# Attention loop of a post-LN layer: value bursts exchanged, the rounding of the maxima on GpSimd, one exponential per score tile

## What is computed

```python
Q = (x @ Wq.T + bq).reshape(b, t, 32, 16).transpose(0, 2, 1, 3)
K = (x @ Wk.T + bk).reshape(b, t, 8, 16).transpose(0, 2, 1, 3)
V = (x @ Wv.T + bv).reshape(b, t, 8, 16).transpose(0, 2, 1, 3)
Q, K = _rope(Q, K)
K, V = jnp.repeat(K, 4, axis=1), jnp.repeat(V, 4, axis=1)
w = jax.nn.softmax(jnp.einsum('bhqd,bhkd->bhqk', Q, K) / 4, axis=-1)
attn = jnp.einsum('bhqk,bhkd->bhqd', w, V)
x = _layernorm(x + attn.transpose(0, 2, 1, 3).reshape(b, t, 512) @ Wo.T + bo)
g = (x @ gate_w.T) * gate_s
u = (x @ up_w.T) * up_s
x = _layernorm(x + (silu(g) * u) @ down_w.T * down_s)
```

## Time and profile before

| | us |
|---|---|
| median of 3 executions | 1063.52 (1063.1 to 1064.48) |
| the profiled execution | 1064.13 |
| its span, first to last instruction | 1062.3 |

### The profile page before, as it was taken

How to read it: one execution, slowest core, us unless ns; L and a number is a source line. 1 busy time by engine, 2 the same in 40 slices (tenths; PEclk the granted TensorE clock), 3 DMA queues, 4 the chain that set the end, 5 groups by cost and what they waited for, 6 DMA issues and landing times.

```text
span 1062.3 us, 15699 instructions
## 1 busy us (share of the span) xinstructions
PE 1026.5 (97%) x5858; PEld 536.8 (51%) x5858; DVE 809.5 (76%) x1199; ACT 665.1 (63%) x1346; POOL 266.2 (25%) x227
## 2 busy tenths in 40 slices
PE   8999999999999999999999999999999999999996
PEld 3643344433443433443444443333337888888885
DVE  4899978899779799779988899999803475662535
ACT  2368877788778788778766678888863431222221
POOL 2751030141335422246200042844100000000002
PEclk9999999999999999999999999999999999999999
DMA  5274417243142512344140446531217510402011
GB/s 200 80 196 126 106 35 213 52 97 78 52 115 75 105 56 54 82 108 105 34 78 12 116 120 150 124 121 37 93 68 193 166 40 9 111 28 52 1 39 42
DMA packets 64432, 94.87 MB, mean 89 GB/s; under 512 B 37536, under 2 KB 37920, under 8 KB 62272
## 3 DMA queue, kind: packets, MB, share of 16 engines
q1 hardware_dynamic: 63776, 93.10, 33.2%
q10 hardware_dynamic: 576, 0.72, 0.2%
HBM read 53.95 MB, written 27.00 MB: 76 GB/s over the span
## 4 chain that ended last, share of the span: by engine, by line
PE 80%; DVE 10%; ACT 6%; issue 2%; DMA 1%; SPq 0%; POOL 0%; DVEq 0%; POOLq 0%
PE PS L448 21%; PE PV L467 20%; PE PSA L537 15%; PE PS L554 5%; PE PSA L426 5%; DVE nmx L964 5%; PE PS L365 4%; ACT Bn L756 3%; PE PS L493 2%; PE PSA L493 2%; DVE nmx L960 2%; DVE nmx L957 2%; ACT Bn L765 2%; PE PV L554 2%; PE PSA L365 1%
## 5 line engine op out<-in xcount | busy, mean ns | idle before, releaser
L756 ACT ACTIVATE Bn<-PS 128x512 f32<-128x512 f32 x1146 | 548.8, 559 | 125.0 <-PE PS L448 111.1
L448 PE MATMUL PS<-Qt,Kt 50*128 50x512 f32 x1146 | 391.7, 434 | 20.0 <-ACT Bn L756 18.7
L426 PE MATMUL PSA<-Kt,Qt 48*128 48x512 f32 x1024 | 390.0, 459 | 2.2 <-DVE Kt L936 0.8
L964 DVE TENSOR_REDUCE nmx<-PSA 128x1 f32<-128x1024 f32 x256 | 312.2, 1219 | 61.0 <-PE PSA L426 59.8
L448 PEld LDWEIGHTS PS<-Qt,Kt 50*128 50x128 f32 x1146 | 184.4, 184 | 323.6 <-ACT Bn L756 312.7
L467 PE MATMUL PV<-Bn 128*32 128x512 f32 x2048 | 272.8, 605 | 0.0
L426 PEld LDWEIGHTS PSA<-Kt,Qt 48*128 48x128 f32 x1024 | 174.6, 183 | 21.7 <-DVE nmx L964 6.2
L960 DVE TENSOR_REDUCE nmx<-PSA 128x1 f32<-128x512 f32 x256 | 174.5, 682 | 1.4 <-PE PSA L426 1.1
L957 DVE TENSOR_REDUCE nmx<-PSA 128x1 f32<-128x512 f32 x256 | 174.3, 681 | 0.0
L537 PE MATMUL PSA<-x1Th,wr 128*128 128x512 f32 x344 | 135.0, 393 | 0.8 <-DVE sg L1052 0.5
L537 PE MATMUL PSA<-x1Tl,wr 128*128 128x512 f32 x344 | 134.7, 392 | 0.0
(11 more groups left out here) (166 smaller groups left out, 919.4 us busy)
## 6 DMA issues: line engine op xcount, KB each, us to landing
Qt<-pscr SPq DMA_DIRECT2D x90, 128.0 KB, 4.9
A<-in_wf SPq DMA_DIRECT2D x11, 768.0 KB, 6.3
wr<-A SPq DMA_DIRECT2D x33, 256.0 KB, 2.9
pscr<-A SPq DMA_DIRECT2D x16, 512.0 KB, 3.7
vscr<-Bn SPq DMA_DIRECT2D x32, 256.0 KB, 2.0
Kt<-pscr SPq DMA_DIRECT2D x90, 64.0 KB, 2.3
A<-A SPq DMA_DIRECT2D x16, 256.0 KB, 3.7
Bn<-vscr SPq DMA_DIRECT2D x8, 512.0 KB
```

The lines of the kernel that those rows point to most:

```text
L426: op = e.matmul(PSA[:, 2 * s + h, :], Qt[n % 3][p:p + NC_, g % 2, 128 * qt:128 * qt + 128], Kt[n % 3][p:p + NC_, 512 * h:512 * h + 512], s ...
L448: e.matmul(PS2[:, i, cols], Kt[n % 3][rows, 128 * kt:128 * kt + 128], Qt[n % 3][rows, g % 2, 512 * qh + cols.start:512 * qh + cols.stop], ...
L756: e.activation(Pb[c % NP_][:, cols], PS2[:, score_bank[c, p], cols], ACT.Exp, scale=0.25).then_inc(*act_exp.next(piece(c, p)))
L964: e.tensor_reduce(nmx[:, hh % 2, c0:c0 + 1], slot_pair(s), AX.XY, ALU.max, negate=True).then_inc(*dve_max[s].next(k))
```

## The change

- The burst moves: `g == (3, 2)[u % 2]`, in an even unit behind S3/M3, in an odd unit behind S2/M2.
- The small piece is gone: every score tile is 512 columns, one product and one exponential, in bank c % 3.
- Background work stands behind the burst of its odd unit, so ahead of S3/M3 instead of behind it. ACT evacuates between the exponentials 2 and 3, and DVE does its part of it between the two half reductions.
- The maxima of half hh, for 1 <= hh < 31, are joined on DVE, rounded and split on GpSimd (`split_max`), and transposed on DVE behind the first reduction of the next half. `write_max` moves from the units v % 8 == 3 to v % 8 == 4 in SP's program.
- The row fetch `gather_at` moves to v == 5. The casts of a rotation move from the 6th and 7th unit behind the projection to the 7th and 9th, which are even units, and the write from the 8th to the 10th.

```diff
-        gather_at = {(n, {0: 13, 6: 5}.get(n, 3)): n + 2 for n in range(NG - 2)}
+        gather_at = {(n, {0: 13}.get(n, 5)): n + 2 for n in range(NG - 2)}
...
-            u0 = 16 * at_u[0] + at_u[1] + 6
-            rope_end.update({divmod(u0, 16): (j, "h0"), divmod(u0 + 1, 16): (j, "h1"), divmod(u0 + 2, 16): (j, "out")})
+            u0 = 16 * at_u[0] + at_u[1] + 7
+            rope_end.update({divmod(u0, 16): (j, "h0"), divmod(u0 + 2, 16): (j, "h1"), divmod(u0 + 3, 16): (j, "out")})
...
+        def apart(hh):
+            return 1 <= hh < 2 * NG - 1
+        def low_max(hh):
+            return (pool_ms if apart(hh) else dve_ms).at(("low", hh))
...
-            return [slice(0, 128), slice(128, 512)] if c % 8 == 3 and c < 4 * SPLIT else [slice(0, 512)]
...
                     scores(u, g)
                     advance(1)
-                    if len(pieces(4 * u + g)) == 2:
-                        scores(u, g, 1)
-                    if u >= 1 and g == (2, 3)[u % 2]:
+                    if u >= 1 and g == (3, 2)[u % 2]:
                         weigh(u - 1)
-                if at_u in project_at:
-                    for h, i in enumerate(free_banks(u)):
-                        project_half(project_at[at_u], h, i, (0, 1, 2, 3))
...
+                        background(u)
...
                 for g in range(4):
                     exponent(u, g)
+                    if g == 2 and at_u in project_at:
+                        for h, i in enumerate(free_banks(u)):
+                            evacuate_raw(project_at[at_u], h, i)
                 if u >= 1:
                     finish(u - 1)
-                if at_u in project_at:
-                    for h, i in enumerate(free_banks(u)):
-                        evacuate_raw(project_at[at_u], h, i)
...
+                if 1 in halves and k % 16 == 15:
+                    join_max(hh)
+                    if not apart(hh):
+                        split_max(hh)
+                        turn_max(hh)
+                if k % 16 == 0 and k > 16 and apart(hh - 1):
+                    turn_max(hh - 1)
...
+            def split_max(hh):
+                top = nmx[:, hh % 2, 0:16]
+                w.wait_ge(*dve_ms.at(("join", hh)))
+                w.wait_ge(*dve_ms.at(("turn", hh - 1)))
+                e.tensor_copy(msp[:, 0:16], top).then_inc(*pool_ms.next(("high", hh)))
+                w.wait_ge(*pool_ms.at(("high", hh)))
+                e.tensor_tensor(msp[:, 16:32], top, msp[:, 0:16].bitcast(F32), ALU.subtract).then_inc(
+                    *pool_ms.next(("low", hh)))
...
+                if u % 8 == 3 and apart(steps_done(u) // 16 - 1):
+                    split_max(steps_done(u) // 16 - 1)
                 if at_u in project_at:
                     rope(project_at[at_u])
...
-                if steps_done(u) // 16 > steps_done(u - 1) // 16:
+                if u % 8 == 4:
                     write_max(steps_done(u) // 16 - 1)
+                if u == SPLIT - 1:
+                    write_max(2 * NG - 1)
```

More of the change, by code:

```diff
@@ L438, in scores @@
                 c = 4 * u + g
-                cols, i = pieces(c)[p], score_bank[c, p]
-                clear(bank_free[i])
+                clear(bank_free[c % 3])
                 w.wait_ge(*max_in[n % 3].at(2 * n + qh))
@@ L751, in exponent @@
                 c = 4 * u + g
[L752 to L757 removed]
+                w.wait_ge(*pe_score.at(c))
+                if c >= NP_:
+                    w.wait_ge(*pe_pv.at((c - NP_) // 4))
+                e.activation(Pb[c % NP_], PS2[:, c % 3, :], ACT.Exp, scale=0.25).then_inc(*act_exp.next(c))
             def finish(u):
```

98 lines of the change are left out of this document (48 added, 50 removed).

## The result

The changed kernel takes **1079.4 us** (median of 4, 1076.94 to 1083.97), the kernel before 1063.37 in the runs beside it. The ratio is 1.0154, with a 95% interval of 1.0115 to 1.0193. It is slower by 1.5%; forecast was 1059.0, in a range from 1049.5 to 1064.0. The profiled execution took 1081.33, with a span of 1079.5.

The account below looks back on a forecast made before the run. It took a cycle of score product, exponential and freed bank between PE and ACT as the bound. Terms -21.3 + 9.1 + 7.7 = -4.5 us on a median of 1063.5 gave 1059.0, range 1049.5 to 1064.0.

Parts of the forecast that it names:

- What bounds the kernel, and the pair: Loop: a cycle of S, exponential, freed bank, next S; without the small piece 0.04 us longer, 4.98 a quiet pair, +4.9.
- The copy: PV copy on ACT fits the gap behind an even unit's burst; 31 copies save 0.50 each, -15.5, less 0.9.
- The turn: Turn of the maxima, partly moved from DVE to GpSimd: 27 turns save 0.43 us each, -11.6.
- rival D: GpSimd's split outlasts its cover, so 30 transposes on DVE come late: slower than before, 1075 at 0.55 each; chance 0.12.
- The sum of the gains: Over the loop's 122 pairs: +4.9, -15.5, -11.6 and +0.9 make -21.3 us.
- The maxima's write behind the broadcast: On SP at five units, held until the broadcast lands: stalls of 2.3 at three, 1.1 at two, +9.1.
- The division: On GpSimd at (12, 11), the split waits behind `divide`, so DVE stands still about 7.7 us: +7.7.
- C: Stalls longer as the maxima's write also shares with 12 fetches: 1063 in the middle, 1068 if all together; chance 0.10.

Follow-up runs that it names:

- the run with both reorderings: Changed kernel, maxima's write ahead of the broadcast at five units, GpSimd's division of (12, 6) behind the split of (12, 11): 1047.52 us, ratio 0.9849.
- the run with the late division: Changed kernel with GpSimd's division of unit (12, 6) moved behind the split of unit (12, 11): 1073.05 us, ratio 1.0084.
- the filled one: Changed kernel with thrown-away products on TensorE ahead of the first score of five stalled units, where PE stood idle: 1071.34 us, ratio 1.0072.

## Why the prediction was wrong

- **What bounds the kernel, and the pair: right.** The cycle S, exponential, freed bank, next S held. Forecast 4.98 a pair, measured 4.99. By the pairs the loss by the small piece is 0.055 x 122 = 6.7 instead of 4.9; taking the piece out of the kernel before, alone, cost 3.5.
- **The copy: right.** It costs nothing in its new place (5.00 against 4.99); the half of 0.06 that I counted, 0.9, wasn't there. By the run with the bursts back it was 14.7, forecast 15.5; the prediction counted 31 copies where the loop has 30.
- **The turn: right in mechanism.** Forecast -11.6, by medians -11.2, by the pairs some 13.6. GpSimd's two operations take 0.20 and 0.22, not the 0.8 each of the earlier trace rows which stood for them as an upper bound. (Nor does the trace show waits inside the records of the earlier trace rows: eight take 0.72 to 0.73 and three 1.03.) From the join's start to the split's end is 0.73 in 29 of the 30 turns (all but (12, 11)), well inside the 1.14 of cover. So rival D was far off: in all of these 29 turns a reduction of 1.16 to 1.22 runs beside the split, and the transpose behind it has no wait. The Trainium skill, "SBUF — State Buffer", section "SBUF: two separate sides", puts the lock on the shared ports on DVE's faster modes and on operations with two inputs in SBUF. These reductions read one input in PSUM, and the trace agrees.
- **The sum of the gains:** forecast -21.3, measured -19.2 as the remainder and -19.1 in the run with both reorderings.
- **The maxima's write behind the broadcast: the mechanism was right, the size not.** Forecast was 2.3 at three units and 1.1 at two, +9.1; measured are 3.72, 4.39, 3.43, 2.65 and 1.45, 15.6. At (6, 8), set against the broadcast's issue, three terms were short: the read went out 6.92 behind it and not 6.1; from the read to the exponential were 2.86 and not 2.4 (of it 0.3 the slow clock); and without the stall the exponential would have come 0.5 to 0.8 earlier than I set it, since the new kernel's units behind the broadcast are quicker.
- **The division: right in mechanism and in the wait.** Forecast +7.7, DVE's wait 7.78, and nothing gave it back. The pair was 9.2 longer, 1.5 more than the wait. In this stretch PE came back at a clock of 0.50; the excess was 1.46 to 1.47 in the three other runs with this stall too (waits of 6.76, 6.99 and 7.11), each time with PE back at 0.50. So it is most likely clock as well; no run had this stall at the full clock.
- **The term that was missing: TensorE's clock.** This is the step that failed: I wrote that nothing would give the stalls back, priced each at its length, and put what comes behind it at nothing, without a reason. In fact PE, idle for 1.47 to 7.30 us, was granted 1.2 GHz behind it, and that cost another 11.4 us in the pairs behind; with the excess of 1.5 at (12, 12), if that is clock too, 12.9. The rows of before held no such idle stretch, and its clock was 1.00 throughout; the granted clock in the earlier trace rows was read as a property of the kernel and not as one that its own idle time could take away. Without the clock the result would have been some 1066 to 1068, outside the range too, and with the stalls as forecast but the clock as it was near 1072 (estimates, from these terms). So either alone made the prediction wrong. None of the rivals had it: C, the longer stalls, came nearest in kind, with 1063 in the middle and 1068 at most; D's 1075 was nearest in time, by a mechanism that wasn't there.
- **The range** was cut on the slow side at C's middle, though five places hung on one guess (how long a small transfer is held) that could only be wrong in the same direction at all of them.

The balance over the loop: with -19.1 for the gain, from the run with both reorderings, -19.1 + 15.6 + 9.2 + 11.4 = +17.1, measured 17.1. Two reorderings remove the last three terms and leave the gain whole, but for the 0.9 at (12, 14).

## What to carry to other kernels

When steps change their place in a queue, ask of each large transfer which small one now stands behind it, and who waits for the small one: here 16 KB waited for 512 KB, five times, and once two operations of 0.2 us on GpSimd stood behind a division that waited for its transfer. Price a stall of TensorE with what comes behind it, too: at the five stalls that a few thrown-away products filled the clock stayed, and each cost only itself. And when a well-argued gain turns into a loss, count first how many pairs are as they should be (here all but twelve), since that separates a wrong idea from a right one with two waits in the wrong order.

## What the runs showed of the hardware

- PE idle for 1.88 us with next to no DMA traffic (a share of 0.03) brought the granted clock to 1.2 GHz behind it, and the next pair took 1.5 us more; idle for 1.25 us in the same run it did not. Other runs cross this order: 0.85 us was enough at (10, 8) of the run with the late division, and 1.61 us at (6, 8) of the filled one was not. So the length of one gap doesn't decide it alone. From 3.13 to 9.42 us of idle time the loss was 1.6 to 3.0, in no order of length.
- A small write on ACT's queue, 1.42 us behind a 512 KB broadcast on SP's, started its first packet after 3.55 us, as the broadcast's last ones ran, and landed in 5.38 us; 0.03 us ahead of one it started after 1.17 and landed in 2.01.
- GpSimd rounds or subtracts 128x16 elements in 0.20 and 0.22 us beside a reduction on DVE; the group of 128x2 at 805 ns in the earlier trace rows, with other operations, is no measure for it.
- Executions of one kernel differ by how long they ran at the low clock: the four of after took 1083.97, 1081.33, 1077.48 and 1076.94 at mean clocks of 0.978, 0.979, 0.981 and 0.982.
